# Scores of an attention kernel: one 128-column matmul each, or four column tiles of 32

## What is computed

```python
q = layernorm(x)                 # (8, 512, 1024)
qh = q.reshape(B, S, KV, G, D).transpose(0, 2, 3, 1, 4)
kh = vh = ctx.reshape(B, S, KV, D).transpose(0, 2, 1, 3)
scores = einsum('bkgsd,bktd->bkgst', qh, kh) / sqrt(D)
out = einsum('bkgst,bktd->bkgsd', softmax(scores), vh)
x = x + out
y = layernorm(x)
# per token: the best of 8 experts by a sigmoid gate on squared projections of y,
# a rank-8 update of that expert, its bias and debias, mixed with y by the gate
x = x + mix(y)
```

## Time and profile before

| | us |
|---|---|
| median of three executions | 1094.2 (1093.95 to 1095.56) |
| profiled execution, its own time | 1095.06 |
| its span, first to last instruction | 1093.2 |

### The profile page before, as it was taken

The page is one execution under the profiler, slowest core; times in us unless marked ns, Lnnn a source line. Parts: engine busy times, 40 slices in busy tenths (PEclk is TensorE's granted clock), DMA queues, the critical chain, the costliest instruction groups (busy, mean ns, idle before and its releaser), DMA issues.

```text
span 1093.2 us, 18664 instructions
## 1 busy us (share of the span) xinstructions
PE 970.6 (89%) x6442; PEld 337.3 (31%) x6442; DVE 919.3 (84%) x1202; ACT 756.3 (69%) x1333; POOL 774.0 (71%) x373
## 2 busy tenths in 40 slices
PE   3269999999999999999999999999999998999994
PEld 2112222222222222222222222222222225776771
DVE  4669999999999899889999999988888874889964
ACT  5348878888788888778878878877767666544430
POOL 2017888888888888888888888888988897111100
PEclk9999999999999999999999999999999999999998
DMA  7744767576767676766666666756455643755322
GB/s 200 203 109 97 163 135 178 136 175 137 172 136 166 133 163 138 165 138 160 143 160 146 164 145 157 156 117 149 105 125 139 154 100 110 248 197 206 139 115 116
DMA packets 324545, 163.88 MB, mean 150 GB/s; under 512 B 187229, under 2 KB 312157, under 8 KB 324453
## 3 DMA queue, kind: packets, MB, share of 16 engines
q1 hardware_dynamic: 324452, 162.70, 60.7%
HBM read 107.84 MB, written 54.53 MB: 149 GB/s over the span
## 4 chain that ended last, share of the span: by engine, by line
PE 45%; DVE 35%; issue 15%; ACT 3%; DMA 1%; POOL 0%; SPq 0%; DVEq 0%; ACTq 0%; POOLq 0%
DVE row_max L809 22%; PE psum L500 10%; PE psum L476 9%; PE psum L488 9%; PE psum L439 5%; PE psum L592 5%; DVE o_t L815 4%; PE psum L573 3%; DVE probs L1004 3%; PE psum L465 2%; DVE prod_mem L868 2%; PE psum L562 1%; DVE stats L837 1%; DMA k_split<-k_parts 1%; DVE k_parts L862 1%
## 5 line engine op out<-in xcount | busy, mean ns | idle before, releaser
L729 ACT ACTIVATE probs<-psum 128x512 f32<-128x512 f32 x1024 | 553.5, 595 | 161.3 <-PE psum L476 156.1
L809 DVE TENSOR_REDUCE row_max<-psum 128x4 f32<-128x2048 f32 x256 | 584.2, 2282 | 39.0 <-PE psum L439 30.5
L280 POOL TENSOR_TENSOR sums<-probs 128x2048 f32<-128x2048 f32 x64 | 290.9, 4546 | 56.6 <-ACT probs L729 56.6
L476 PE MATMUL psum<-q_stack,k_stack 97*128 97x512 f16 x1024 | 317.9, 386 | 12.5 <-ACT probs L729 10.2
L292 POOL TENSOR_TENSOR sums<-probs 128x2048 f32<-128x2048 f32 x64 | 291.6, 4556 | 26.0 <-ACT probs L729 26.0
L488 PE MATMUL psum<-probs,v_in 128*32 128x512 f32 x2048 | 273.6, 606 | 5.1 <-ACT probs L729 2.6
L476 PEld LDWEIGHTS psum<-q_stack,k_stack 97*128 97x128 f16 x1024 | 78.3, 97 | 254.0 <-ACT probs L729 147.0
L439 PE MATMUL psum<-high_mem 32*128 32x512 f16 x1024 | 103.1, 391 | 39.3 <-DVE row_max L809 28.3
L500 PE MATMUL psum<-sums,ones 128*32 128x512 f32 x1024 | 121.6, 592 | 0.0
L821 DVE STREAM_TRANSPOSE den_t<-psum 128x512 f32<-128x512 f32 x64 | 45.9, 717 | 64.7 <-PE psum L500 64.7
L256 POOL TENSOR_TENSOR o_t<-o_t,inv 128x512 f32<-128x512 f32 x64 | 67.2, 1049 | 37.5 <-DVE inv L827 37.5
(11 more groups left out here) (93 smaller groups left out, 703.1 us busy)
## 6 DMA issues: line engine op xcount, KB each, us to landing
q_stack<-q_split SPq DMA_DIRECT2D x192, 128.0 KB, 3.3
xa<-in_x_dram SPq DMA_DIRECT2D x32, 512.0 KB, 3.6
q_split<-prod_mem SPq DMA_DIRECT2D x16, 1024.0 KB, 5.6
o_all<-in_x_dram SPq DMA_DIRECT2D x256, 64.0 KB, 2.3
x_attended<-o_all SPq DMA_DIRECT2D x64, 256.0 KB, 4.4
out_dram<-probs SPq DMA_DIRECT2D x32, 512.0 KB, 2.9
high_mem<-q_split SPq DMA_DIRECT2D x64, 128.0 KB
high_mem<-k_split SPq DMA_DIRECT2D x64, 128.0 KB
```

The costliest lines, as they stand in the source:

```text
L280: pool.tensor_tensor(sums[:, (2 * u - 1) % SUMS], probs[:, (u - 1) % 2, 2], probs[:, (u - 1) % 2, 3], ALU.add).then_inc(back_done, 1)
L476: pe.matmul(st_ps[:, bank_of["score", u, n], :], k_stack[:, u % SLOTS, t * P:(t + 1) * P], q_stack[:, u % SLOTS, g, :], start=True, stop=T ...
L729: act.activation(probs[:, s, t, g, :], st_ps[:, bank_of["score", u, n], :], ACT.Exp, scale=EXP_SCALE).then_inc(exped, 1)
L809: dve.reduce_max(row_max[:, u % 2, t:G * ST:ST], s_ps[:], AX.X).then_inc(reduced, 1)
```

## The change

`score_keys` makes each score in four matmuls instead of one. Each takes 32 of the 128 keys as its stationary columns, streams the same 512 queries, and writes 32 partitions of the same bank. The last one carries the semaphore. The rest of the program is the same; lines below it move by 3.

```diff
                     for g in (2 * pair, 2 * pair + 1):
                         n = t * G + g
                         bank_free("score", u, n)
-                        pe.matmul(st_ps[:, bank_of["score", u, n], :], k_stack[:, u % SLOTS, t * P:(t + 1) * P],
-                                  q_stack[:, u % SLOTS, g, :], start=True, stop=True).then_inc(scored, 1)
+                        for row in range(0, P, D):
+                            last = pe.matmul(st_ps[row:row + D, bank_of["score", u, n], :],
+                                             k_stack[:, u % SLOTS, t * P + row:t * P + row + D],
+                                             q_stack[:, u % SLOTS, g, :], start=True, stop=True)
+                        last.then_inc(scored, 1)
```

## The result

The changed kernel takes 1082.8 us (median of five executions; 1094.2 before). The ratio is 0.9887, with a 95% interval from 0.9872 to 0.9902, so it is faster by 1.0 to 1.3%. Measured again beside the experiments it took 1082.2 us, ratio 0.9898 (0.9877 to 0.9918). The prediction was 1079.7, with a range from 1073 to 1091.

A forecast was written before the change was run, and what follows sets the result against it. VectorE was taken to bound most steps, TensorE only the denominators' step (t = 3). Saving 63 x 0.23 = 14.5 us from 1095.06 gave 1080.6 profiled; with the median 0.9 lower, 1079.7 us, range 1073 to 1091.

The forecast's parts named there:

- TensorE sets the end in the step with the denominators alone: At t = 3 TensorE sets the end, VectorE in nearly all other steps; shortening those gains nothing.
- A switch of tiling costs 0.10 to 0.14, and a neighbour of the same tiling nothing: On TensorE: 0.10 to 0.11 us for a pair of scores, 0.14 for products; changing type or row count alone costs nothing.
- Four float16 tiles run at once, a set in 0.215: Scores on TensorE: a set of four column tiles takes 0.215 us, half a float32 set; two sets take 0.43.
- The slower case: Rival: four float16 tiles don't run at once; at 0.43 us a set some 80 us lost, 1175; chance 0.18.
- instructions that come too slowly: Rival: TensorE's instructions can't keep pace; at 0.06 us a matmul, 6.3 us of the gain go, 1086.0; chance 0.06.
- The two switches that the trace didn't hold, between row and column tiles: Around score_rows: each assumed to cost like other switches, giving 0.33 and 0.55 us, with bounds of 0.10 either way.
- The rival of the double price: A switch between row and column tiles costs double: 9.5 us of 14.5 go, 1089.2; chance 0.10.
- No cost at t = 2: Around the maxima's transpose TensorE loses some 0.07 us, hidden by a 0.22 cover; uncovered, 1.8 us over 26 steps.
- The sum, 63 x 0.23 = 14.5: Denominators' step saves 0.23 us (4.12 to 3.89) in each of 63 units in the loop, 14.5 us in all.
- All of it lies on the path: In the denominators' step, the whole 0.23 us saved was claimed to shorten the critical path.
- The first rival: Row-column switches cost double; the step's beginning is covered by a bank wait in odd units; 1089.2; chance 0.10.
- What would show it: Profile signs: pair 0.43, products 0.86, denominators' step 3.89; VectorE's 64.7 us wait falls some 8; start spread over 0.02 refutes.

The follow-up runs named there:

- t3only: Changed kernel with column tiles only in step t = 3 (the denominators' step), whole-array scores elsewhere: 1081.9 us, ratio 0.9892 to the kernel before.
- not_t3: Changed kernel with column tiles only in steps t = 0 to 2, whole-array scores at t = 3: 1093.2 us, ratio 0.9992 to the kernel before.
- half64: Changed kernel with each score in two column tiles of 64 keys instead of four of 32: 1098.0 us, ratio 1.0039 to the kernel before.
- short_exp: Changed kernel, odd units from 3 on: exponentials of groups 2 and 3 at t = 2 cover only 256 queries, leaving work out; 1078.1 us, ratio 0.9847.

## Why the prediction was right, and where its size was off

The time came within the range, 3.1 us above the forecast: 11.4 us were gained where 14.5 were predicted. The mechanism holds, and one term of the sum was too large.

- *TensorE sets the end in the step with the denominators alone*: shown, but for t = 0 of the eleven units without an input tile (0.9 us). t3only has the whole gain, not_t3 none that the time can tell.
- *A switch of tiling costs 0.10 to 0.14, and a neighbour of the same tiling nothing*: shown by the even step (3.88, forecast 3.89), term by term within 0.02. By distances of starts the two switches that went cost 0.09 (0.54 to 0.45) and 0.11 (1.83 to 1.72); the 0.14 came from the chain, which cuts the time elsewhere. half64 shows that it is the switch. (The "0.11 each" of rows 2 and 4 is the difference between them: in rows 4 there is no switch.)
- *Four float16 tiles run at once, a set in 0.215*: right. Pair to products is 0.45 (forecast 0.43), and the rows of eight scores last 0.62, less one's 0.38 it is 0.24: 0.215 and the spread. In the step with the denominators the four starts of a set lie within 0.02 us, and the next set starts some 0.22 later. The slower case didn't come, nor that of instructions that come too slowly, though rows 7, named against the latter, show only weight loads.
- *The two switches that the trace didn't hold, between row and column tiles*: 0.32 from score_rows to the first pair and 0.54 from the second pair to score_rows, as before. I had taken the middle of the bounds by likeness alone; no row showed it. The rival of the double price is out.
- *No cost at t = 2*: nearly. In an even unit it is 0.20 from the maxima's transpose to the second pair (414.95 to 415.15; before, 420.20 to 420.32, 0.12), and the wait for VectorE behind it hides that. In the 26 odd units with an input tile 0.03 to 0.04 come through to the next step (t3only, not_t3): 1 us, where the prediction priced an uncovered loss at 1.8.
- *The sum, 63 x 0.23 = 14.5*: **mis-sized**. The step that failed is "All of it lies on the path", which I read in an even unit and multiplied by all 63. In the 26 odd units with an input tile the saving is 0.12. There score_rows doesn't wait for VectorE at t = 3, so that the first pair comes sooner behind the scores of the step before (403.89 less 402.79 is 1.10, against 1.25 in the even unit, 416.40 less 415.15); its bank, and the products behind it, wait for ScalarE's exponentials. I had seen that wait as a cover for the loss at t = 2, and not that the same wait, one step on, caps the gain. The first rival even says that the step begins under a wait for a bank in odd units, but the sum didn't use it. With it the sum is 37 x 0.23 + 26 x 0.12 = 11.6, or 12.5 with the 0.9 at t = 0, against 11.4 (1094.2 less 1082.8) and 11.9 measured. short_exp shows the cause: it gives back the missing half.
- *What would show it*: two of the signs I named were wrong. The chain gives the pair 0.55, not 0.43: behind score_rows there is still a switch, as in the 0.54 of before, so that 0.43 should never have been expected of it; the start distances are the right measure. VectorE's wait before the denominators fell by 4.8 us, not 8: 0.12 in the even units, 0.01 in the odd ones with an input tile. And a sign of being wrong came in part, without harm: outside the step with the denominators, 168 of the 1024 sets have starts spread by more than 0.02, up to 0.048. No set in that step has.

## What to carry to other kernels

Where small matmuls in column tiles stand beside whole-array ones, bring the neighbours to the same tiling, to the same width. Count only the switches in steps that TensorE sets, since here three quarters of the tiled scores gave nothing in sum. Before multiplying a step's saving by the number of units, look at one unit of each kind: what hides a loss at one place can cap the gain at the next. Where a step's neighbour has idle time on TensorE, work that can be cut in two can move there: here that gave 9.5 us by itself, beside some 12 for the switches, and 21 together (1094.55 to 1073.58).

## What the runs showed of the hardware that was not expected

In this trace a column tiling of 64 beside one of 32 costs as much as the whole array beside it: 0.56 us from a pair of scores to the products, against 0.54 from the whole array and 0.45 from tiles of 32. And a pair of scores keeps its pace whether it is made by two matmuls of 128 columns, four of 64 or eight of 32: first start to last end is 0.60, 0.62 and 0.62 us, with eight weight loads passing in 0.12 us.
